# One block for all stages up to the sampling and one behind it: waits on producers in place of barriers, norms begun early

## What is computed

```python
x = x + L0_conv(_ln_c(x))    # batch norm, linear attention with two heads, gates
t = tokens(x); t = t + L0_ffn(_ln_t(t))   # 16 experts of 128, SwiGLU, best two
x = x + L1_conv(_ln_c(x))    # 3x3 convolution, kernel mixed from 8 by routing
t = t + L1_ffn(_ln_t(t))     # 8 experts of 256, exact GELU, best two
x = x + L2_conv(_ln_c(x))    # 5x5 and dilated 3x3 depthwise with dynamic taps
t = t + L2_ffn(_ln_t(t))     # as L1
x = x + L3_conv(_ln_c(x))    # deformable 3x3 convolution, group norm, relu
t = t + L3_ffn(_ln_t(t))     # as L0
def _ln_c(v, eps=1e-06):     # _ln_t is the same over a token's 64 channels, eps 1e-05
    m = jnp.mean(v, axis=1, keepdims=True); s = jnp.var(v, axis=1, keepdims=True)
    return (v - m) / jnp.sqrt(s + eps)
```

## Time and profile before

| | us |
|---|---|
| median of 3 runs | 1872.83 (1870.38 to 1875.67) |
| the profiled execution's own time | 1870.68 |
| its span, first to last instruction | 1868.5 |
| mean granted clock of PE, share of full speed | 0.963 |
| busy: PE, DVE, ACT, POOL | 1686.5, 1100.9, 977.6, 879.3 |

### The profile page before, as it was taken

One profiled execution on the slowest core, in us unless ns is written; L12 is line 12 of the kernel. 1 busy time (PEld: TensorE's weight loads), 2 busy tenths in 40 slices (PEclk: granted clock), 3 DMA queues, 4 the chain that ended last, 5 costly groups with the idle time before them and its releaser, 6 DMA issues. The chain is left out here.

```text
span 1868.5 us, 31745 instructions
## 1 busy us (share of the span) xinstructions
PE 1686.5 (90%) x11879; PEld 947.2 (51%) x11879; DVE 1100.9 (59%) x1526; ACT 977.6 (52%) x1426; POOL 879.3 (47%) x736
## 2 busy tenths in 40 slices
PE   6879999998579999877999977999999759999998
PEld 2635555554234444333444434777777525555554
DVE  5667777765863432365344245656656466777765
ACT  3454555554136666516666643666666445455554
POOL 1418877776024333312333335333333008778777
PEclk8989999999799999999999988999999979999999
DMA  5014333334102322301222230000000004333333
GB/s 119 1 24 104 114 105 108 109 107 129 29 1 77 88 81 78 84 1 28 88 80 66 91 93 1 2 1 2 1 2 1 3 1 116 110 112 122 112 113 98
DMA packets 71584, 121.43 MB, mean 65 GB/s; under 512 B 16962, under 2 KB 18690, under 8 KB 70786
## 3 DMA queue, kind: packets, MB, share of 16 engines
q1 hardware_dynamic: 71426, 119.32, 21.8%
HBM read 115.60 MB, written 3.67 MB: 64 GB/s over the span
## 5 line engine op out<-in xcount | busy, mean ns | idle before, releaser
L675 POOL TENSOR_TENSOR x<-x,mx_gated 128x512 f32<-128x512 f32 x256 | 331.4, 1295 | 94.2 <-DVE mx_gated L630 92.8
L623 DVE TENSOR_TENSOR mx_hidden<-mx_second,mx_hidden 128x1024 f32<-128x1024 f32 (+1 forms) x256 | 245.0, 957 | 179.0 <-PE mx_second L502 179.0
L778 ACT ACTIVATE mx_hidden<-mx_first,w_bias 128x1024 f32<-128x1024 f32 x256 | 264.5, 1115 | 124.8 <-PE mx_first L502 124.8
L821 POOL TENSOR_TENSOR x<-x,mx_gated 128x512 f32<-128x512 f32 x128 | 164.6, 1286 | 260.4 <-DVE mx_gated L795 260.4
L795 DVE SCALAR_TENSOR_TENSOR mx_gated<-mx_out,w_bias,mx_gates 128x512 f32<-128x512 f32 x128 | 96.0, 750 | 286.7 <-PE mx_out L752 265.3
L607 ACT ACTIVATE mx_hidden<-mx_first 128x1024 f32<-128x1024 f32 x256 | 248.6, 1022 | 18.6 <-PE mx_first L502 4.5
L571 PE MATMUL mx_out<-mx_hidden,w_second 128*64 128x512 f32 x1024 | 249.3, 606 | 5.6 <-issue 3.8
L1761 DVE TENSOR_TENSOR c_near_weights<-c_near_hats 128x768 f32<-128x768 f32 x192 | 190.0, 1037 | 103.1 <-PE c_near_turned L1632 103.0
L502 PE MATMUL mx_first<-tokens_high,w_high 64*128 64x512 f32 x1024 | 217.4, 420 | 21.6 <-PEq L64 21.3
L752 PE MATMUL mx_out<-mx_hidden,w_second 128*64 128x512 f32 x1024 | 233.4, 599 | 0.0
L599 ACT COPY mx_kept<-mx_second 128x512 f32<-128x512 f32 x128 | 75.3, 588 | 266.1 <-PE mx_second L502 266.1
(11 more groups left out here) (235 smaller groups left out, 2232.8 us busy)
## 6 DMA issues: line engine op xcount, KB each, us to landing
mx_gates<-gate_board SPq DMA_DIRECT2D x768, 128.0 KB, 3.1
w_first<-in_f_first SPq DMA_DIRECT2D x4, 1024.0 KB, 12.1
c_weight<-in_c_weight SPq DMA_DIRECT2D x1, 2304.0 KB
x<-in_x SPq DMA_DIRECT2D x8, 256.0 KB, 4.7
w_second<-in_f_second SPq DMA_DIRECT2D x4, 512.0 KB, 13.4
w_first<-in_f_first SPq DMA_DIRECT2D x4, 512.0 KB, 10.0
out_x<-x SPq DMA_DIRECT2D x16, 128.0 KB, 2.6
gate_board<-xn SPq DMA_DIRECT2D x16, 64.0 KB, 2.8
```

The lines of the kernel that those rows point to most:

```text
L623: dve.tensor_tensor(own, second[:, 0:halves, :], own, ALU.mult).then_inc(s.hidden.semaphore, 1)
L675: pool.tensor_tensor(place, place, gated[:, n % GATED, :], ALU.add).then_inc(s.added.semaphore, 1)
L778: act.activation(hidden[:, n % HIDDEN, f], first[:, (n * F + f) % BLOCKS], ACT.Gelu, bias=w.bias1[:, e * F + f:e * F + f + 1]).then_inc(s. ...
L821: pool.tensor_tensor(place, place, gated[:, n % GATED, :], ALU.add).then_inc(s.added.semaphore, 1)
```

## The change

Everything up to conv3's sampling is one block, `sample_near` and `sample_rest` keep theirs, and all behind them is one block; POOL is no longer drained at their ends. A stage's function adds its instructions to the block that is open. Where a barrier ordered things, an instruction now waits for the semaphore of its producer: the convs for `s.normed` of the chunks that they read, a mixture's first product for the weights' low parts, the logits and the tokens' low parts, `batch_norm`'s users for `scaled`, of which there is one for each image. PSUM is one tensor `k.ps` of eight banks, out of which each stage takes its own by number; the squares have an own room in SBUF, deviations and scales lie in `k.gate`.

The norm becomes a class. Its head (products of chunks 0 to 3, their squares, the first variance, deviation and scale, two copies) is issued at the end of the stage before, on each engine behind that stage's own instructions; the first norm has it at its start. The order in the norm changes: the first variance stands before the fourth product, the first deviation before the fourth square, and DVE takes the second scale before the third copy. The last add of each mixture moves from POOL to DVE, and in the SwiGLU mixtures the odd second half of the last product as well. In the tail of a SwiGLU mixture a product of the next norm's head stands ahead of the last second layer. In conv2 ACT sums three images instead of two, in `offsets` ACT copies three instead of two, so that DVE has one.

```diff
-def layer_norm(k, turn, eps, loads, router=None, stats=None):
+class Norm:
+    def head_tensor(self, pe, ready, start=0, end=4):
+        for i in range(start, end):
+            ready(i)
+            self.centre(pe, i)
+            if i == 2:
+                self.variances(pe, 0)
+    def head_scalar(self, act):
+        act.activation(self.k.spare[:, 0:1], self.k.eps[self.eps][:], ACT.Sqrt)
+        self.square(act, 0)
+        self.square(act, 1)
+        self.keep(act, 0)
+        self.square(act, 2)
+        self.deviations(act, 0)
+        self.square(act, 3)
+        self.keep(act, 1)
+    def head_vector(self, dve):
+        self.centres(dve, 0)
+        self.centres(dve, 1)
+        self.scales(dve, 0)
...
-        block = ctx.enter_context(nc.Block())
+        block = k.block
...
-            centres(0)
-            centres(1)
-            scales(0)
-            centres(2)
-            scales(1)
-            scales(2)
-            norm(0)
-            centres(3)
-            norm(1)
-            scales(3)
+            if turn == 0:
+                m.head_vector(dve)
+            m.scales(dve, 1)
+            m.centres(dve, 2)
+            m.norm(dve, 0)
+            m.scales(dve, 2)
+            m.centres(dve, 3)
+            m.norm(dve, 1)
+            m.scales(dve, 3)
...
+    def add_last(self, dve, x, gated):
+        steps = CHUNKS * self.E
+        self.s.gated.wait(dve, steps)
+        self.s.added.wait(dve, steps - 1)
+        place = x[:, chunk(CHUNKS - 1)]
+        dve.tensor_tensor(place, place, gated, ALU.add).then_inc(self.s.added.semaphore, 1)
...
+        if following:
+            following.head_tensor(pe, ready, 0, 1)
         second_layer(STEPS - 1)
         third_layer(STEPS - 2)
+        if following:
+            following.head_tensor(pe, ready, 1, 2)
         third_layer(STEPS - 1)
+        if following:
+            following.head_tensor(pe, ready, 2, 4)
...
-            dve.tensor_scalar(xn[:], xn[:], both[:, 5:6], both[:, 7:8], ALU.mult, ALU.add)
+        for j in range(IMAGES):
+            image = xn[:, j * PIX:(j + 1) * PIX]
+            dve.tensor_scalar(image, image, both[:, 5:6], both[:, 7:8], ALU.mult, ALU.add).then_inc(s.scaled, 1)
...
             for j in range(IMAGES):
+                act.wait_ge(k.ln.normed, normed + 2 * (j + 1))
                 act.copy(padded[:, j, 1:1 + H, 1:1 + W], image[:, j]).then_inc(s.padded, 1)
...
         y = sb("y", [P, N])
+        k.part.close()
         sample_near(k, w_deform, coords, base, ints, y)
...
+        open_part(k)
+        group_norm(k, y, pairs, gn_gamma, gn_beta, Norm(k, turn + 1, 1e-5))
```

More of the change, by code:

```diff
@@ new lines, in wide_of, with centre, variances @@
+    def wide_of(self, n):
+        return self.wide if n < self.PAIRS - 1 else self.mean[:, 0:2, :]
+    def centre(self, pe, i):
+        k, s, n = self.k, self.s, i // 2
+        if n >= 2:
+            pe.wait_ge(s.squared, self.chunks + i - 3)
+            pe.wait_ge(s.kept if i % 2 else s.centred, self.pairs + n - 1)
+        pe.matmul(self.mean[:, i % 4, :], k.centring[:], k.x[:, chunk(i)], start=True, stop=True).then_inc(s.mean, 1)
+    def variances(self, pe, n):
+        k, s = self.k, self.s
+        pe.wait_ge(s.squared, self.chunks + 2 * n + 2)
+        if n >= 1:
+            pe.wait_ge(s.dev, self.pairs + n)
+        for q in range(4):
+            last = pe.matmul(self.var[self.quarter(q), 0:self.COLS], k.averages[:],
+                             k.square[:, (2 * n + q // 2) % 4, self.columns(q)], start=True, stop=True)
+        last.then_inc(s.var, 1)
@@ new lines, in spreads @@
+    def spreads(self, pe, n):
+        k, s = self.k, self.s
+        pe.wait_ge(s.scale, self.pairs + n + 1)
+        if n == self.PAIRS - 1:
+            pe.wait_ge(s.kept, self.pairs + n)
+            pe.wait_ge(s.centred, self.pairs + n)
+        elif n >= 1:
+            pe.wait_ge(s.normed, self.chunks + 2 * n)
+        for q in (0, 2, 1, 3):
+            last = pe.matmul(self.wide_of(n)[:, q // 2, self.columns(q)], k.spreading[half(q // 2), q % 2, :],
+                             k.scale[half(q // 2), n % 2, :], start=True, stop=True)
+        last.then_inc(s.wide, 1)
@@ L100, in _ @@
                     load_image(k, sp, j)
+            elif not router:
+                k.mx.added.wait(sp, 0)
             for to, source, semaphore in loads:
```

494 lines of the change are left out of this document (261 added, 233 removed).

## The result

The changed kernel takes 1825.84 us (median of 4 runs, 1824.15 to 1827.32) against 1874.25 for the kernel before (4 runs on the same chip, 1870.38 to 1878.24): a ratio of 0.9738, 95% interval 0.9717 to 0.9758. The profiled execution took 1824.15 us with a span of 1822.4, so 46.2 us of span are gone (1868.55 to 1822.36) where my sum had 55.7. The forecast of 1817 was 9 us too low; the range held the time.

The account below looks back on a forecast made before the run. TensorE, busy 90% of the span, was taken as the bound, with the gain at the seams: 33.0 + 4.5 + 7.8 + 10.0 + 2.0 - 1.6 = 55.7 us off the 1868.5 span, so 1817 us predicted, range 1804 to 1836.

Parts of the forecast that it names:

- Heads of the norms: At seven seams between stages, the next norm's start up to its first reciprocal overlaps the last adds: 33.0 us gained.
- Rest of the norms: Behind the heads DVE is the limit and the new order keeps it fed: 0.6 to 0.7 in each of seven, 4.5.
- Router to mixture: Four seams: PE needs only logits, but ACT's activation waits for the tanh: 1.9 per GELU, 2.0 per SwiGLU mixture, 7.8.
- Starts of the convs: Conv1 1.55 plus 0.3, conv3 3.1, conv2 1.1 plus 0.3 plus 3.6 from a POOL-DVE collision going away: 10.0 gained.
- Conv0: POOL's early weight split collides with DVE's batch-norm steps, PE starting at 40.9 instead of 39.43: net loss of 1.6 us.
- End: The last mixture has the same tail as the others, with no product inserted: 2.0 us gained.
- Rival (a): The collision of POOL's split with DVE's steps in conv0 doesn't come: 5.7 us more gained, 1811 us, chance 0.13.
- Rival (b): Heads don't hold, PE and ACT late: seven seams give back 1.5 to 2.5 each, conv2's collision stays; 1835, chance 0.2.
- a sign of being wrong: What would show the forecast wrong: half-clock products in the heads, reciprocals of more than 1.75 us, or longer mixtures.
- (c): Waits put in place of barriers give no overlap; only the barriers' 0.3 us for 18 blocks go: 1867 us, chance 0.02.
- (d): Slower: without barriers, more DVE choice steps in four mixtures are caught under POOL, 1.0 us each: 1917 us, chance 0.02.
- The opening: Norm behind the first mixture: PE busy 15.9 of 21.4 us, much of that as half-clock products with nobody else feeding them.

Follow-up runs that it names:

- e7_squash_later: The changed kernel with ScalarE's tanh of the first gates put behind the first two experts' activations in all four mixtures: 1825.61 us.

## Why the prediction was right, and where not

- **Heads of the norms**, 33.0 worked out, 34.2 measured. Each to 0.3 us, save behind conv3 (5.3 worked out, 5.9 measured). The mechanism was right, but the sum didn't price its parts: overlap 18.1 (3.2 of it the clock), order 8.6, of which the rest of the norms gives back 4.2, and the last add on VectorE 6.9 behind three mixtures (5.1 of it the clock).
- **Rest of the norms**, 4.5 worked out, -4.4 measured: the term that failed. The step was that behind the head DVE is the limit and the new order keeps it fed, for 0.6 to 0.7 us in each of seven norms. It holds where there is no router (0.5 to 0.6 each). With a router I had counted only VectorE's instructions. The changed kernel has TensorE's fourth variance behind `route(0)`, so the fourth deviation comes late, and ScalarE's table load, two high parts and the copy follow that deviation; TensorE's fourth spreading is queued behind them. With the copy early, 5.6 of the 6.0 us came back, 1.0 of it by the clock. The rule of naming who is queued behind each waiting instruction would have found it.
- **Router to mixture**, 7.8 worked out, 6.8 measured: 1.5 and 1.1 in the SwiGLU mixtures, instead of 2.0, where TensorE's products behind its wait of 4.74 us take 0.63 us instead of 0.40 up to 134.5 in the first; 1.7 and 2.4 in the GELU ones. The order of waits was right: the first expert product stands 0.1 us behind the last logits (542.73 against 542.63), ScalarE's first activation comes 2.1 us earlier behind them than before, TensorE stops for 2.5 us at the ring of buffers, and e7_squash_later showed the choice to bind next.
- **Starts of the convs**, 10.0 worked out. Conv1's start gained 1.83 (1.85 worked out), and its products took 0.9 less (32.54 us at a granted clock of 0.96, before 33.45 at 0.93). Conv2 gained 4.3 of 5.0: the collision went, as said, and is worth 3.0 instead of 3.6; that it went was a matter of 0.3 us. Conv3 gained 4.8 instead of 3.1: the start as said, and 2.8 that I hadn't seen, because its 288 products no longer begin at half clock (15.68 us at a granted clock of 1.00, against 18.44 at 0.85). Of that 1.1 is lost again, since POOL's split, now later against the offsets, catches one step:

```profile
1077.30 15.68 PE L1623 MATMUL ps<-c_padded,c_w_off 64*32 64x512 f32 x288
...
1088.35 9.91 POOL L453 TENSOR_TENSOR w_low<-w_first,w_high 128x512 fp32r<-128x512 f32 x8
...
1097.04 1.23 DVE L1660 SCALAR_TENSOR_TENSOR c_reach<-c_reach 128x1 f32<-128x1 f32 x1
```

That the sum of the convs came out (10.8 against 10.0) is partly luck: 2.8 and 0.9 us of clock that I hadn't worked out cover what the collisions cost.

- **Conv0**, -1.6 worked out, -3.0 measured. The collision came as described, at a smaller price on VectorE (the key products start at 39.77, not 40.9: not every step is caught for a whole POOL instruction). What I left out is the clock: kept waiting 2.4 us, TensorE runs the key products 2.8 us longer. Against my sum that is 1.1 better and 2.8 worse.
- **End**, 2.0 against 1.9.
- Rival (a) fell with conv0. Rival (b) named the right place for what went wrong, work behind an early head, at 2.1 us at most in four norms and not in seven, and with another engine: ScalarE's queue, not a late head. Half-clock products in the heads, which I had named as a sign of being wrong, did not appear behind mixtures. Behind conv3 they did (first eight in 6.55 us, before in 6.70), and the head gained 5.9 us all the same. (c) and (d) found nothing: from the seventeenth gated product to the eighth last the mixtures took the same in both kernels to 0.02 us (259.5 or 259.6 us with SwiGLU, 135.7 with GELU). The 1917 us of (d) doesn't follow from its own figures: 204 steps at 1.0 us would be 204, not 100.
- The opening says that much of TensorE's work in the norm behind the first mixture runs at half clock. The granted clock of 0.92 in the earlier trace rows makes that some 3.4 of 21.4 us (an estimate from the two levels), so the clock was a small part of that stretch.

## What to carry to other kernels

When barriers go and instructions are reordered, redo the timeline of every engine through the stage, not only that of the engine that was the limit: here the limit moved to a copy of 0.37 us that sat behind a table load. Work that starts early because nothing holds it any more lands beside something: look up what each small step on VectorE reads, and hold POOL's long instructions back if its steps have two inputs in SBUF. Where two edits cure the same wait, keep the one nearer its source, and look whether the change itself made the wait, as the moved variance did here.

## What the runs showed of the hardware

- The granted clock of a seam isn't settled by that seam: the same eight centring products behind waits of 2.91 and 2.92 us took 3.70 us in one kernel (granted 1.00) and 5.38 in the other (0.68). Filling a wait with idle products set the clock right there (5.40 to 3.70 us at both places) and gained nothing in the time (1853.16 against 1852.53 us, one run each).
- While POOL subtracts, a one-column step with two inputs on VectorE is stretched from 0.16 to as much as 1.19 us, and a scaling of 1024 columns from 0.81 to 1.75; a reciprocal with one input isn't (0.16 on one column, 1.75 on 256 beside POOL's casts). POOL's subtractions beside the scaling went from 1.26 to 1.71 us.
